# Row chunks for a second layer norm, one PSUM bank for the attention transposes, and new order lists in a two-layer graph kernel

## What is computed

```python
# layer 0: 4 heads of 64
q, k, v = split_heads(h @ Wq), split_heads(h @ Wk), split_heads(h @ Wv)
attn = softmax(where(adj, q @ k.T / 8, -max))
x = x + (attn @ v) @ Wo + bo
# layer 1: 8 heads of 64; sm is adj: where it is true, it masks
m = h @ map_w.T + map_b
n = m / max(norm(m), 1e-8)                     # per head
cos_adj = (n @ n.T * ~sm) > 0.1
q, k = m @ q_w.T + q_b, m @ k_w.T + k_b
p = softmax(where(sm, -1e10, q @ k.T / 8)) * keep     # keep = ~sm[:, 0]
a = cos_adj * p
out = relu((a @ (h @ gcn_map_w.T + b)) @ gcn_W.T / (a.sum(-1) + 1))
x = x + out
```

## Time and profile before

| | us |
|---|---|
| median of 3 executions | 4123.62 |
| lowest, highest | 4120.02, 4124.43 |
| the profiled execution | 4121.26 |
| its span, first to last instruction | 4119.5 |
| PE busy | 3931.4 (95%) |
| VectorE busy | 2608.3 (63%) |
| ScalarE busy | 1979.3 (48%) |
| GpSimd busy | 1324.3 (32%) |

### The profile page before, as it was taken

The page is one execution under the profiler, slowest core; times in us unless marked ns, Lnnn a source line. Parts: engine busy times, 40 slices in busy tenths (PEclk is TensorE's granted clock), DMA queues, the critical chain, the costliest instruction groups (busy, mean ns, idle before and its releaser), DMA issues.

```text
span 4119.5 us, 105002 instructions
## 1 busy us (share of the span) xinstructions
PE 3931.4 (95%) x32976; PEld 3437.0 (83%) x32976; DVE 2608.3 (63%) x9426; ACT 1979.3 (48%) x5583; POOL 1324.3 (32%) x2007
## 2 busy tenths in 40 slices
PE   7999999999999999999999999999999999999997
PEld 6888888888888888888888888888888888888886
DVE  4666666666666666666666666666666666666664
ACT  3554544544545445445454454454454544544544
POOL 3333333333332333333333333333333333333332
PEclk8999999999999999999999999999999999999998
DMA  3000000000000000000000000000000000000000
GB/s 87 16 32 26 22 32 16 32 32 16 32 27 21 32 18 30 32 16 32 29 18 32 22 25 32 16 32 32 16 32 27 21 32 16 32 32 16 32 27 17
DMA packets 65544, 111.77 MB, mean 27 GB/s; under 512 B 20880, under 2 KB 22448, under 8 KB 65520
## 3 DMA queue, kind: packets, MB, share of 16 engines
q1 hardware_dynamic: 64928, 110.12, 7.8%
q0 software_dynamic: 592, 1.35, 0.2%
HBM read 44.34 MB, written 33.55 MB: 19 GB/s over the span
## 4 chain that ended last, share of the span: by engine, by line
PE 65%; DVE 12%; issue 11%; ACT 6%; POOL 4%; DVEq 1%; DMA 1%; POOLq 0%; ACTq 0%; SPq 0%
PE bank L755 34%; PE bank L763 9%; PE bank L748 7%; PE bank L783 6%; PE bank L775 4%; ACT prob L501 3%; PE bank L883 3%; POOL prob L417 2%; DVE x_mid L663 2%; ACT att L475 2%; DVE prob L650 2%; DVE att L607 2%; DVE att L618 1%; POOL rstd L362 1%; DVE hT L640 1%
## 5 line engine op out<-in xcount | busy, mean ns | idle before, releaser
L475 ACT ACTIVATE att<-att,nmax 128x256 f32<-128x256 f32 x1024 | 509.7, 500 | 299.6 <-DVE nmax L607 299.6
L417 POOL TENSOR_SCALAR prob<-prob,rsum 128x256 f32<-128x256 f32 x512 | 241.1, 487 | 631.2 <-DVE rsum L657 628.2
L755 PE MATMUL bank<-hT,w_qkv 128*128 128x256 f32 x3072 | 414.9, 288 | 4.7 <-DVE hT L640 4.7
L755 PE MATMUL bank<-qkm,w_k 128*128 128x256 f32 x3072 | 416.6, 285 | 0.0
L755 PEld LDWEIGHTS bank<-hT,w_qkv 128*128 128x128 f32 x3072 | 376.9, 189 | 37.9 <-issue 24.2
L755 PE MATMUL bank<-hT,w_map 128*128 128x256 f32 x3072 | 396.7, 285 | 5.1 <-DVE hT L640 1.0
L618 DVE SCALAR_TENSOR_TENSOR att<-bank,att 128x256 f32<-128x256 f32 x1024 | 392.3, 420 | 4.0
L755 PE MATMUL bank<-qkm,w_q 128*128 128x256 f32 x3072 | 390.8, 283 | 0.0
L755 PEld LDWEIGHTS bank<-hT,w_map 128*128 128x128 f32 x3072 | 372.5, 189 | 18.4 <-DVE hT L640 17.3
L763 PE MATMUL bank<-w_v,hT 128*128 128x512 f32 x1536 | 385.3, 399 | 0.0
L755 PEld LDWEIGHTS bank<-qkm,w_k 128*128 128x128 f32 x3072 | 380.1, 188 | 5.0
(11 more groups left out here) (122 smaller groups left out, 7949.6 us busy)
## 6 DMA issues: line engine op xcount, KB each, us to landing
x_in<-x SPq DMA_DIRECT2D x64, 512.0 KB, 3.4
x_res<-x_mid SPq DMA_DIRECT2D x64, 512.0 KB, 3.1
...
```

The source lines that it names most:

```text
L417: last = g.tensor_scalar(prob0[:, hd, c, :], prob0[:, hd, c, :], rsum0[:, hd, c:c + 1], 0.0, ALU.mult, ALU.add)
L475: s_.activation(e_sl, e_sl, ACT.Exp, bias=nmax1[:, p, c, e:e + 1], scale=-1.0, accum_out=esum1[:, p, c, e:e + 1]).then_inc(exp1_done, 1)
L755: last = t_.matmul(dst, w(ws, k)[:, t * 128:t * 128 + 128], rhs[:, rs, k, :], start=(k == 0 and i == 0), stop=(k == KT - 1 and i == 2))
```

## The change

The semantics and the instructions stay; three things and the orders differ.

1. The layer norm helpers work on one row chunk: `row_stats(k, src, c)` does the statistics and the mean of chunk c, `rstd_of(k, c)` does `var_e` and `pow` on one column, `normalise(k, src, c)` one chunk. For the second layer norm the lists hold `rstd1a`, `rstd1b`, `norm1a`, `norm1b`; the first one still does both chunks in one step. A `ht` step now transposes one row chunk (all four column blocks) where it transposed two column blocks of both rows, so `ht1a` needs only `norm1a`; but `qk` and `m` steps need both `ht` steps from their first matmul.
2. Transposes of `att` (turn_a and turn_b), value and back all use bank 4. turn_a of a pair waits until the previous pair's back is read (`rel_done`), turn_b until turn_a is copied. Score waits only for the masked reads of the pair before, cos only for the gated ones.
3. String products rotate over three banks (5 to 7) in place of four.

```diff
     TENSOR = [
-        "ht0a", ("score", 0), "ht0b", ("cos", 0), "qk0", "qk1", ("turn_a", 0), "qk2", ("turn_b", 0), "s0", "s1", ("value", 0),
-        "qk3", ("back", 0), ("score", 1), ("cos", 1), "s2", "s3", "pt0", "v0", "pt1", ("turn_a", 1), ("turn_b", 1), "pt2",
-        "pt3", ("value", 1), "av", ("back", 1), ("score", 2), ("cos", 2), "wo0", "wo1", ("turn_a", 2), ("turn_b", 2),
-        ("value", 2), ("score", 3), ("back", 2), "ht1a", "ht1b", ("cos", 3), "m0", "m1", "m2", ("turn_a", 3), ("turn_b", 3),
-        "m3", ("value", 3), "vv0", "ss", "q2", "q1", "q0", "k1", ("back", 3), "rt", "k0", "q3", "k3", "bc0", "bc1", "k2",
-        "vv1"
+        ("score", 0), "ht0a", "ht0b", ("cos", 0), ("score", 1), "qk0", ("turn_a", 0), "qk1", "qk2", "qk3", ("turn_b", 0), "s0",
+        "s1", ("cos", 1), ("score", 2), ("value", 0), "s2", "s3", ("back", 0), "v0", "pt0", ("turn_a", 1), "pt1", "pt2", "pt3",
+        ("turn_b", 1), ("cos", 2), "av", ("value", 1), ("score", 3), ("back", 1), "wo0", ("turn_a", 2), "wo1", ("turn_b", 2),
+        ("cos", 3), ("value", 2), "ht1a", ("back", 2), "ht1b", ("turn_a", 3), "m0", "m1", "m2", ("turn_b", 3), "m3",
+        ("value", 3), "vv0", "ss", "q1", "q2", "q3", ("back", 3), "rt", "q0", "k0", "bc0", "k3", "k1", "bc1", "k2", "vv1"
     ]
     SCALAR = [
-        ("unit", 0), "ht0a", "ht0b", ("exp_a", 0), ("exp_b", 0), "qk0", "qk1", ("turn_a", 0), ("unit", 1), "qk2",
-        ("turn_b", 0), "exp0", ("value", 0), "exp1", "qk3", ("exp_a", 1), ("exp_b", 1), "exp2", "exp3", "pt0", "pt1",
-        ("turn_a", 1), ("turn_b", 1), "pt2", "pt3", ("value", 1), "av", ("exp_a", 2), ("exp_b", 2), ("turn_a", 2),
-        ("turn_b", 2), ("value", 2), "ht1a", "ht1b", ("exp_a", 3), "m0", ("exp_b", 3), "m1", ("turn_a", 3), "m2",
-        ("turn_b", 3), "m3", "q2", ("value", 3), "q1", "k1", "q0", "k0", "q3", "k3", "k2"
+        ("unit", 0), "ht0a", "ht0b", ("exp_a", 0), ("exp_b", 0), "qk0", "qk1", "qk2", ("turn_a", 0), ("exp_a", 1),
+        ("exp_b", 1), ("turn_b", 0), ("unit", 1), "qk3", "exp0", ("value", 0), "exp1", "exp2", "exp3", "pt0", ("turn_a", 1),
+        "pt1", "pt2", "pt3", ("exp_a", 2), ("turn_b", 1), ("exp_b", 2), "av", ("value", 1), ("exp_a", 3), ("turn_a", 2),
+        ("turn_b", 2), ("value", 2), "ht1a", "ht1b", ("exp_b", 3), ("turn_a", 3), "m0", "m1", "m2", ("turn_b", 3), "m3",
+        ("value", 3), "q1", "q2", "q3", "q0", "k0", "k3", "k1", "k2"
     ]
     VECTOR = [
-        "ht0a", "ht0b", ("score_a", 0), ("score_b", 0), ("cos_a", 0), "qk0", ("cos_b", 0), "qk1", "s0", "qk2", "s1",
-        ("factor", 0), "sum0", ("back", 0), "sum1", "qk3", ("score_a", 1), ("score_b", 1), "s2", ("cos_a", 1), "s3",
-        ("cos_b", 1), "sum2", "sum3", "v0", ("factor", 1), ("back", 1), "av", ("score_a", 2), ("score_b", 2), ("cos_a", 2),
-        ("cos_b", 2), "wo0", "wo1", "norm1", ("factor", 2), ("back", 2), "ht1a", "ht1b", ("score_a", 3), ("score_b", 3),
-        ("cos_a", 3), "m0", ("cos_b", 3), "m1", ("factor", 3), "stats0", "m2", "m3", "ss", "vv0", "q1", "q2", "q0", "k1", "rt",
-        ("back", 3), "k0", "norm0", "q3", "k3", "k2", "bc0", "bc1", "vv1"
+        ("score_a", 0), ("score_b", 0), "ht0a", "ht0b", ("cos_a", 0), ("cos_b", 0), "qk0", "qk1", ("score_a", 1),
+        ("score_b", 1), "qk2", "s0", "qk3", "s1", "sum0", ("cos_a", 1), ("factor", 0), "s2", "sum1", "s3", "sum2", ("back", 0),
+        "sum3", "v0", ("cos_b", 1), ("score_a", 2), ("cos_a", 2), ("score_b", 2), ("factor", 1), ("cos_b", 2), "av",
+        ("factor", 2), ("score_a", 3), ("back", 1), ("score_b", 3), "wo0", "wo1", "norm1a", "norm1b", ("cos_a", 3),
+        ("back", 2), "ht1a", "ht1b", ("cos_b", 3), "m0", "m1", "stats0", "m2", ("factor", 3), "norm0", "m3", "vv0", "ss", "q1",
+        "q2", "q3", ("back", 3), "rt", "q0", "k0", "bc0", "k3", "k1", "k2", "bc1", "vv1"
     ]
     POOL = [
-        ("unit", 0), "mid", "mask0", "sum0", "sum1", ("unit", 1), ("back", 0), "sum2", "sum3", "rstd1", ("back", 1),
-        ("back", 2), "m0", "rstd0", "m1", "m2", "m3", "pow", "mask1", ("back", 3)
+        "mid", ("unit", 0), "mask0", ("unit", 1), "sum0", "sum1", "sum2", "sum3", ("back", 0), "rstd1a", "rstd1b", ("back", 1),
+        "m0", "rstd0", "m1", "mask1", "m2", "m3", ("back", 2), "pow", ("back", 3)
     ]
-    PBANKS = 4
+    PBANKS = 3
     SYNC = [
         "x", ("out", 0), "move", "adj"
     ]
     PRODUCTS = [s for s in TENSOR if isinstance(s, str)]
-    bank_of = {s: 4 + k % PBANKS for k, s in enumerate(PRODUCTS)}
+    bank_of = {s: 5 + k % PBANKS for k, s in enumerate(PRODUCTS)}
...
-        score_bank, gram_bank, t_bank = bank[0:2], bank[2:4], bank[0:2]
-        v_bank = gram_bank
+        score_bank, gram_bank, t_bank = bank[0:2], bank[2:4], (bank[4], bank[4])
+        v_bank = t_bank
...
-            def rstd_of(k):
-
-                pool.wait_ge(stat_done, 4 * k + 4)
+            def rstd_of(k, c):
+
+                pool.wait_ge(stat_done, 4 * k + 2 * c + 2)
                 pool.sem_inc(passed_gpsimd, 1)
-                g.tensor_scalar(var_e[:, :], mv[:, :, 1], 1.0, LN_EPS, ALU.mult, ALU.add).then_inc(var_done, 1)
-                pool.wait_ge(var_done, 2 * k + 1)
+                g.tensor_scalar(var_e[:, c:c + 1], mv[:, c, 1:2], 1.0, LN_EPS, ALU.mult, ALU.add).then_inc(var_done, 1)
+                pool.wait_ge(var_done, 4 * k + 2 * c + 1)
                 pool.sem_inc(passed_gpsimd, 1)
-                g.tensor_tensor(rstd[:, :], var_e[:, :], minus_half[:, 0:C], ALU.pow).then_inc(var_done, 1)
+                g.tensor_tensor(rstd[:, c:c + 1], var_e[:, c:c + 1], minus_half[:, c:c + 1], ALU.pow).then_inc(var_done, 1)
...
-            def row_stats(src, c):
+            def row_stats(k, src, c):
 
                 v_.bn_stats(stats[:, c, :], src[:, c, :]).then_inc(stat_done, 1)
-
-            def mean_var(k):
-
-                for c in range(C):
-                    dve.wait_ge(stat_done, 4 * k + c + 1)
-                    dve.sem_inc(passed_vector, 1)
-                    v_.bn_aggr(mv[:, c, :], stats[:, c, :]).then_inc(stat_done, 1)
-
-            def normalise(k, src):
-
-                dve.wait_ge(var_done, 2 * k + 2)
-                for c in range(C):
-                    v_.tensor_scalar(h[:, c, :], src[:, c, :], mv[:, c, 0:1], rstd[:, c:c + 1], ALU.subtract, ALU.mult).then_inc(h_ready, 1)
+                dve.wait_ge(stat_done, 4 * k + 2 * c + 1)
+                dve.sem_inc(passed_vector, 1)
+                v_.bn_aggr(mv[:, c, :], stats[:, c, :]).then_inc(stat_done, 1)
+
+            def normalise(k, src, c):
+
+                dve.wait_ge(var_done, 4 * k + 2 * c + 2)
+                v_.tensor_scalar(h[:, c, :], src[:, c, :], mv[:, c, 0:1], rstd[:, c:c + 1], ALU.subtract, ALU.mult).then_inc(h_ready, 1)
...
-                        t = 2 * "ab".index(kind[3])
+                        rows = slice(128 * "ab".index(kind[3]), 128 * "ab".index(kind[3]) + 128)
                         act.wait_ge(product_full, in_psum(n, kind))
-                        s_.activation(flat(hT[:, 0, t:t + 2, :]), bank[bank_of[kind]][:, :], ACT.Relu).then_inc(high_done, 1)
+                        s_.activation(hT[:, 0, :, rows], bank[bank_of[kind]][:, :].rearrange("p (k i) -> p k i", i=128),
+                                      ACT.Relu).then_inc(high_done, 1)
...
-                        pe.wait_ge(uT_ready, pairs(a, p, 2))
+                        pe.wait_ge(masked, pairs(a, p, 4))
                         head_products(score_bank, q1[:, :, p, :], k1[:, :, p, :])[1].then_inc(score_full, 1)
                     elif kind == "cos":
                         pe.wait_ge(nlow_done, 2 * a + 2 + p // 2 + 1)
-                        pe.wait_ge(rel_done, pairs(a, p))
+                        pe.wait_ge(gated, pairs(a, p, 4))
                         head_products(gram_bank, nrm[:, :, p, :], nrm[:, :, p, :])[1].then_inc(gram_full, 1)
                     elif kind in ("turn_a", "turn_b"):
                         e = "ab".index(kind[5])
                         pe.wait_ge(gated, pairs(a, p, 4) + 2 * e + 2)
+                        if e == 0:
+                            pe.wait_ge(rel_done, pairs(a, p))
+                        else:
+                            pe.wait_ge(uT_ready, pairs(a, p, 2) + 1)
                         transposes(t_bank[e], lambda jc, c: att[:, p % 2, e, c, jc * 128:jc * 128 + 128]).then_inc(t_full, 1)
...
-                        pe.wait_ge(h_ready, 4 * n + (2 if kind[2] == "0" else 4))
-                        empty(n, kind)
-                        transposes(full, lambda k, c: h[:, c, (t + k) * 128:(t + k + 1) * 128]).then_inc(product_full, 1)
+                        c = "ab".index(kind[3])
+                        pe.wait_ge(h_ready, 4 * n + (1 if kind[2] == "0" else 3) + c)
+                        empty(n, kind)
+                        transposes(full, lambda k, half: h[:, c, (2 * k + half) * 128:(2 * k + half) * 128 + 128]).then_inc(product_full, 1)
                     elif kind[:2] == "qk":
```

(6 more changed lines are left out.)

47 lines of the change are left out of this document (22 added, 25 removed).

## The result

The changed kernel takes 4294.1 us (median of 4 runs, 4284.1 to 4297.9) against 4124.0 (4120.0 to 4125.4): 1.041 times as long, 95% interval 1.039 to 1.043. The forecast was 4142 with a range of 4080 to 4180. The direction was the likelier one, the size was missed by 152 us, and the time lies outside the range. The profiled execution took 4284.1 us, its span is 4282.2, and the mean clock that TensorE was granted in it is 0.963 of full speed, where the execution of before had 0.993. This last number, the granted clock, is the one to read first.

The account below looks back on a forecast made before the run. The prediction took TensorE, with a matmul under way in 95% of the span, as the bound. +32 us over 63 periods, -6 for the last graph and -5 for the first gave 4121.3 + 21 = 4142 us, range 4080 to 4180.

Parts of the forecast that it names:

- Norm 0 among the m's: Statistics, rstd, norm0 and mask1 delay the squares m2 and m3: stall before ss of 0.25 to 0.9 us, taken as 0.5.
- Removed waits: PE's waits on uT and prob go, 1.16 us a period won; margins about 0.2 at pt3 and pt2, 0.35 at av.
- The second rival: Margins of three banks and one transpose bank break, at pt1 to turn_b 1 and av: 4174 us; chance 0.15.
- The chain of the second layer norm: From wo1 to m0 6.6 us, 4.15 covered by work: 2.4 us stall before ht1b, turn_a 3 and m0, against 2.5.
- A: Start of the second x_mid addition, from which the second layer norm's steps are counted; m0 can start 6.4 us later.
- Norm first, GpSimd second: In the second layer norm, VectorE's norm holds up GpSimd's var_e until it ends: 0.37 us, bounds nothing or 0.37.
- forecast's sign of being wrong: In the second layer norm, var_e starting 0.2 us after the mean with norm1a under way.
- The first rival: No hold from VectorE to GpSimd: second layer norm stall 2.0 us, total 4104 us, or 4091 with faster pow; chance 0.28.
- qk0: The first projections wait for ht0b, with VectorE reading scores ahead of it: 0.38 us of stall.
- Start and end: First graph -5 us (between 0 and -8.5), where s2 waited for qk3; last graph -6 us, where pairs take less time.
- A period: Sum for one graph: work +0.05, new stalls 3.3 us against 2.8, so +0.5 us, times 63 = +32 us.

Follow-up runs that it names:

- before_squares2: The kernel before, with two useless GpSimd multiplications of 216 columns ahead of its last square, so PE stalls before ss; 4233.3 us, ratio 1.0265.
- ss_behind_q1: The changed kernel with ss moved behind q1 on PE and VectorE; 4210.8 us, ratio 1.0214.
- wide_ss: The changed kernel with each matmul of ss streaming 64 columns in place of 2, the stall kept; 4204.5 us, ratio 1.0206.
- norm0_late: The changed kernel with norm0 moved back behind k0 on VectorE and mask1 behind pow on GpSimd; 4129.3 us, ratio 1.0020.
- no_chunks: The changed kernel with the row chunks of layer norm and h transposes undone, its banks and order lists kept; 4216.8 us, ratio 1.0228.
- cos_in_gap: hold_short with VectorE's cos_a 3 moved between norm1a and norm1b; 4065.2 us, ratio 0.9859.
- hold_short: norm0_late with GpSimd's x_res addition of pair 1 moved ahead of both rstd steps; 4085.8 us, ratio 0.9907.
- hT_first: hold_short with cos_a 3 and back 2 behind ht1a and ht1b on VectorE, turn_a 3 behind m0 on PE and ScalarE; 4168.8 us, ratio 1.0109.

## Why the prediction was wrong, step by step

**The step that failed** is one that the prediction never put down as a step: that a stall of PE costs its own length, at full clock. Under "Norm 0 among the m's" it foresaw the stall in front of `ss` and priced it at 0.5 us, 32 us in all. The stall is 0.76 idle, 0.92 from start to start (2045.10 to 2048.93 is 3.83; before it was 2.91 for the same group, 2033.92 to 2036.83 in the timeline of the kernel before, below), so the size was at its upper bound of 0.9: the two engines hold each other there, as feared. In 62 graphs one of norm0's passes takes 0.84 us in place of 0.54, mask1 0.74 in place of 0.62 and one of the small ones 0.36 in place of 0.18. That alone is 63 x 0.42 = 26 us over the sum. But behind it stood w_q's 91 us, 75 of which before_squares2 shows with a stall of 0.23, and no case of the sum, the rivals or the range had it. Without the clock the changed kernel would have come at 4294 - 122 = 4172, inside the range.

```profile
2033.92 3.06 PE L763 MATMUL bank<-w_v,hT 128*128 128x512 f32 x12
2036.83 1.84 PE L883 MATMUL bank<-half_of,ptm 128*128 128x2 f32 x16
2038.53 4.50 PE L755 MATMUL bank<-qkm,w_q 128*128 128x256 f32 x36
```

Nothing in the trace of before showed this price, because nothing stalled in front of `ss` there. It even spoke for the assumption: PE stood still 1.36 us in front of the transposes of `h` and 0.74 in front of value 2, once a graph, and the clock fell in none of the 62. A stall that had cost its own length was taken to cost that anywhere. The trace did show what a reader could have asked: which of the new stalls stands next to a group of sixteen matmuls of two columns? The prediction used the lower clock in one place, the last graph, and did not ask where else it could fall. The Trainium skill's page on TensorE, named above, could have made a rival of its own out of that question (its section Part 1: The HAM clock gate has the clock set by how busy PE has been); the prediction did not weigh it.

**The rest of the sum, point by point:**

- *Removed waits*: right. Of the waits on `uT` 3.8 us in 5 pieces are left in the whole run, of those on `prob` none. The margins on pt3, pt2 and av held: no wait of PE on them. The second rival is out.
- *The chain of the second layer norm*: 2.4 us of stall forecast; from turn_b 2, the group behind wo1, to m0 6.62 us pass (2031.15 to 2037.77), with the forecast's 4.15 of work about 2.5. Three pieces of about 0.9, 0.5 and 0.9 forecast, 0.96, 0.39 and 0.47 idle measured. From A (2031.50) to m0 are 6.27 us; forecast 6.4.
- *Norm first, GpSimd second*: the hold is there, but its price of 0.37 was too much. `var_e` starts 0.2 us after its mean, in the middle of the norm, and takes 0.33 in place of 0.19. It ends at 2033.79, and the norm at 2033.74: in all 64 graphs it ends 0.05 us after the norm. So GpSimd's step gets through only once the norm has ended, as the forecast had it, but by then it has most of its own time behind it, and the hold costs 0.14. The forecast's sign of being wrong, `var_e` starting 0.2 after the mean, looked at the start, and the row shows the hold only in the end.

```profile
2033.08 0.18 DVE L538 BATCH_NORM_AGGREGATE mv<-stats 128x2 f32<-128x6 f32 x1 [0.15 <-DVE stats L535]
2033.19 0.55 DVE L543 TENSOR_SCALAR h<-x_mid,mv,rstd 128x512 f32<-128x512 f32 x1
...
2033.46 0.33 POOL L358 TENSOR_SCALAR var_e<-mv 128x1 f32<-128x1 f32 x1 [0.84 <-DVE mv L538]
2033.97 0.56 POOL L361 TENSOR_TENSOR rstd<-var_e,minus_half 128x1 f32<-128x1 f32 x1 [0.18 <-POOL var_e L358]
2034.49 0.72 POOL L410 TENSOR_TENSOR x_res<-x_res,rel 128x256 f32<-128x256 f32 x1
...
2034.56 0.94 DVE L543 TENSOR_SCALAR h<-x_mid,mv,rstd 128x512 f32<-128x512 f32 x1 [0.82 <-POOL rstd L361]
```

 The other direction is as the earlier trace rows had it: `x_res` first, and the norm takes 0.94. The one-column pow takes 0.55, as worked out from the earlier trace rows. A term was left out, a wait of 0.15 between statistics and mean in each chunk, which about makes up for what the hold did not take. The Trainium skill's rule (SBUF — State Buffer, Who interferes with whom) agrees with the trace for GpSimd first, and for VectorE first too: `var_e` ends 0.05 us behind the norm. The first rival, no hold, had the mechanism wrong, and its 2.0 for the chain did not come.
- *qk0*: 0.38 forecast; 2004.81 to 2006.01 is 1.20, where score groups that stand side by side take 0.81 to 0.91, so about 0.35.
- *Start and end*: -5 and -6 forecast, -5.2 and -6.8 measured. In the last graph there is no norm0, and so neither the stall nor the fall of the clock:

```profile
4230.49 1.84 PE L878 MATMUL bank<-half_of,ptm 128*128 128x2 f32 x16
4232.19 4.50 PE L750 MATMUL bank<-qkm,w_q 128*128 128x256 f32 x36
```

- *A period*: +0.5 forecast, +0.89 measured at full clock, nearly all of the difference from the term for `ss` (0.92 in place of 0.5).

**What stays open.** In which graphs the clock falls at `ss` cannot be read from the stall. At 533.84 the changed kernel has the same stall, and the projections run at full clock; but in this graph the clock had fallen at m0 already, 12.7 us before:

```profile
521.15 6.06 PE L750 MATMUL bank<-hT,w_map 128*128 128x256 f32 x36 [0.47 <-DVE hT L637]
...
533.84 1.94 PE L878 MATMUL bank<-half_of,ptm 128*128 128x2 f32 x16 [0.77 <-DVE v L680]
535.64 4.50 PE L750 MATMUL bank<-qkm,w_q 128*128 128x256 f32 x36
```

All but two of the 62 graphs are like that: one fall each, at one site or the other. In most of the runs with falls they come in a regular rhythm, every third graph, every second, four of five, so it seems to count when in time a stall comes, and not only how long it is and what stands behind it. No run varied that by itself, so this rival is left standing: where a change also shifts the stalls in time, part of what the clock then does may be luck.

Nor is it shown why two of the repairs at `ss` raised w_map (ss_behind_q1, wide_ss) and the third (norm0_late) did not. And the sites differ: at `ss` 0.23 us brought it about in 49 graphs (before_squares2) and 0.34 in none (no_chunks). At m0 0.56 and 0.97, the latter behind eight transposes (cos_in_gap), did nothing, 0.57, 0.39 and 0.47 (hold_short) still cost w_map 15 us, and 0.57 and 1.41 (hT_first) 75, each against w_map's 397.3 in cos_in_gap; 1.36 in front of eight transposes did nothing in the kernel before.
